# Passage from attention to the expert tiles: eight pieces of work put in another order or on another engine

## The reference, cut to what matters

```python
attn_out = _mha(x, in_proj_w, in_proj_b, out_proj_w, out_proj_b)
x = _layernorm(x + attn_out, ln1_g, ln1_b)
gp = softmax(xt @ w_group + b_group); g_idx = argmax(gp)          # 4 groups
ep_sel = softmax of the 2 experts of that group; e_idx_local = argmax
combine = one_hot(flat_e, 8) * (g_prob * e_prob)
h = relu(xt @ w1[e] + b1[e]); y = h @ w2[e] + b2[e]; out = combine @ y
x = _layernorm(x + moe_out, ln2_g, ln2_b)                          # and the input x is added
```

## Time and profile before

| | us |
|---|---|
| median of 3 runs | 595.16 |
| lowest, highest | 593.21, 599.90 |
| the profiled execution: its time | 594.82 |
| the profiled execution: its span | 593.0 |
| self-attention's last turn ends, first tile's result on DVE (in the span) | about 492, 506.1 |

### The profile page before, as it was taken

One profiled execution on the slowest core, in us unless ns is written; L12 is line 12 of the kernel. 1 busy time (PEld: TensorE's weight loads), 2 busy tenths in 40 slices (PEclk: granted clock), 3 DMA queues, 4 the chain that ended last, 5 costly groups with the idle time before them and its releaser, 6 DMA issues. The chain is left out here.

```text
span 593.0 us, 14386 instructions
## 1 busy us (share of the span) xinstructions
PE 517.6 (87%) x4673; PEld 345.3 (58%) x4673; DVE 430.0 (73%) x1165; ACT 396.4 (67%) x1109; POOL 286.7 (48%) x511
## 2 busy tenths in 40 slices
PE   6888799999999999989799998999998757987780
PEld 4656466777666666654455555555555436766660
DVE  3697978888888888857455678686777758955662
ACT  4456578877887888885576776766776544656660
POOL 0577742222222222020533568686786462766564
PEclk9997999999999999999999999999999898689886
DMA  8600999999996000000100000101220043243410
GB/s 331 270 2 30 278 269 275 272 272 274 272 275 176 0 0 0 2 1 4 34 2 2 1 3 29 38 29 45 103 97 28 29 118 83 78 126 96 106 39 10
DMA packets 48534, 60.76 MB, mean 102 GB/s; under 512 B 2488, under 2 KB 45509, under 8 KB 47574
## 3 DMA queue, kind: packets, MB, share of 16 engines
q1 hardware_dynamic: 45686, 53.59, 33.2%
q0 software_dynamic: 2784, 6.37, 3.1%
HBM read 18.30 MB, written 42.10 MB: 102 GB/s over the span
## 5 line engine op out<-in xcount | busy, mean ns | idle before, releaser
L1567 DVE TENSOR_REDUCE nm<-SC 128x8 f32<-128x1024 f32 x64 | 75.3, 1219 | 30.4 <-PE SC L1076 29.8
L1464 DVE TENSOR_REDUCE room_w<-SC 128x512 f32<-128x2048 f32 x32 | 73.3, 2290 | 13.7 <-PE SC L927 13.7
L2081 ACT ACTIVATE room_p<-ST 128x1024 f32<-128x1024 f32 x64 | 62.1, 1021 | 22.8 <-PE ST L1094 22.8
L600 POOL TENSOR_TENSOR spread<-parts,units 128x48 bf16<-128x48 bf16 x32 | 8.8, 275 | 122.8 <-DVE parts L1454 122.8
L1987 ACT ACTIVATE room_w<-room_w,shift 128x128 f32<-128x128 f32 x128 | 49.8, 391 | 20.6 <-DVE shift L1471 20.4
L798 POOL DMA_INDIRECT out<-room_v,id_r x39 | 39.2, 1004 | 23.9 <-DVE room_v L1915 13.8
L1978 ACT ACTIVATE room_w<-ST,cv 128x128 f32<-128x128 f32 x128 | 36.5, 367 | 17.3 <-PE ST L942 17.2
L1113 PE MATMUL SC<-room_p,room_w 128*32 128x128 f32 x1024 | 35.6, 281 | 7.6 <-DVE room_w L1592 4.1
L942 PEld LDWEIGHTS ST<-room_w 128*128 128x128 f32 x256 | 33.1, 191 | 15.4 <-issue 13.0
L2088 ACT ACTIVATE room_w<-SC 128x512 f32<-128x512 f32 x32 | 19.1, 598 | 33.9 <-PE SC L1113 33.1
L1996 ACT ACTIVATE room_w<-room_w,inv 128x128 f32<-128x128 f32 x128 | 41.0, 409 | 0.6 <-DVE inv L1476 0.6
(11 more groups left out here) (297 smaller groups left out, 1401.2 us busy)
## 6 DMA issues: line engine op xcount, KB each, us to landing
sorted_rows<-w SPq DMA_DIRECT2D x8, 4290.0 KB, 42.2
room_v<-sorted_rows SPq DMA_DIRECT2D x39, 130.0 KB
x_t<-xT SPq DMA_DIRECT2D x2, 1024.0 KB, 8.1
ctx_t<-adj SPq DMA_DIRECT2D x1, 2048.0 KB, 17.3
room_w<-x SPq DMA_DIRECT2D x8, 256.0 KB, 2.9
room_w<-mask SPq DMA_DIRECT2D x1, 1536.0 KB
w<-weights SPq DMA_DIRECT2D x1, 1228.0 KB, 8.5
x_t<-w SPq DMA_DIRECT2D x1, 1032.0 KB, 6.4
```

The source lines that it names most:

```text
L1464: dve.tensor_reduce(logit[:, :, :], SC[:, :, :].rearrange("p b (i m) -> p b m i", i=TYPES), AX_X, ALU.max)\
L1567: dve.tensor_reduce(nm[:, v % 2, 2 * PER_R * pair:2 * PER_R * (pair + 1)], SC[:, 2 * pair:2 * pair + 2, :].rearrange("p r (i n) -> p (r i) ...
L2081: act.activation(ex[:, v % 2, 2 * pair:2 * pair + 2, :], ST[:, 2 * pair:2 * pair + 2, :], ACT.Exp)\
```

## The change

1. POOL: `rows_x(6)`, until now on DVE at the end of turn 31, is done by POOL in `rest(0)`.
2. DVE: `first_taken` moves from the end of turn 31 to the end of turn 29.
3. DVE: `norm1_logits(6)` and links 0 to 5 move from turn 32 behind `normalise(31)`, `residual_out(29)` and its statistics; links 6 to 11 move from there behind `residual_out(30)`.
4. DVE: `norm1_logits(7)` moves from `rest(3)` to ahead of `rows_x1(6)`.
5. PE: the rank product of group 6 moves from turn 1 to turn 2 of the tile pipeline, behind the first tile's `ht`.
6. ACT: `norm1_out(6)` moves behind the copy of the first tile, `gate_exps(6)` to the end of turn 2.

```diff
 # GpSimd
             def rest(k):
+                if k == 0:
+                    rows_x(G - 2)
                 if k == 1:
                     norm1_power(G - 1)
 # TensorE
             def ranks(k):
-                if k == 1:
+                if k == 2:
                     pe.wait_ge(S("route_chain"), (G - 3) * ROUTE + RANK_LINK)
                     rank(G - 2, False)
...
-                if k == 1:
+                if k == 2:
                     ranks(k)
 # VectorE
-                if b == 0 and normed:
+                if b == 0 and normed and u < B:
                     norm1_logits(norm)
                     route(norm, range(0, 6))
...
-                if u == B - 1:
-                    rows_x(G - 2)
+                if u == B - GB + 1:
                     first_taken()
             def rest(k):
...
                     norm1_stats(B - 3)
-                    route(G - 2, range(6, 12))
+                    norm1_logits(G - 2)
+                    route(G - 2, range(0, 6))
                 if k == 1:
                     residual_out(B - 2)
                     norm1_stats(B - 2)
+                    route(G - 2, range(6, 12))
                 if k == 2:
...
                     route(G - 2, range(12, SLOT_LINK))
+                    norm1_logits(G - 1)
                     rows_x1(G - 2)
                 if k == 3:
-                    norm1_logits(G - 1)
                     route(G - 2, range(SLOT_LINK, ROUTE))
 # ScalarE
                 if k == 1:
                     heads_turned(B - 1)
+
+            def later_rest(k):
+                if k == 1:
                     norm1_out(G - 2)
+                if k == 2:
                     gate_exps(G - 2)
-            def later_rest(k):
```

## The result

| | before | after |
|---|---|---|
| median of 20 runs each, us | 594.38 | 597.14 |
| lowest, highest | 592.13, 599.90 | 591.91, 600.23 |
| profiled execution: time, span | 594.82, 593.0 | 594.2, 592.4 |

The ratio is 1.0041, 95% interval 1.0022 to 1.0059: slower by 2.4 us (0.0041 x 594.38), against +0.8 forecast. The case within 1% came true, and so did the wide range of 590.5 to 600.0 us; on the forecast's base the ratio gives 597.3 us (1.0041 x 594.82), just above its own range of 594.5 to 597. The profiled pair shows the opposite sign, 592.4 against 593.0 us, and can't be read by its spans: the executions differ in the tile loop by more than the change does. The profiled execution of the changed kernel is also 2.9 us faster than its median. So the passage is read by itself, from one place that the change doesn't touch, `residual_out(25)`, to DVE's first result.

What follows compares the result with a forecast made beforehand. No engine bounds throughout: DVE and PE lead by turns, nobody from 480 to 490. `first_taken` +1.30 and residuals -0.5, the rest 0, gave +0.8 on 594.82: 595.6 us; own range 594.5 to 597, wide range 590.5 to 600.0.

Steps and rivals of the forecast that it cites:

- The case within 1%: Whole kernel: time differs by no more than 1% (5.9 us), about what a measurement can tell; chance 0.89.
- `first_taken` to turn 29: DVE, ahead of `normalise(28)` and `residual_out(26)`: no cover while PE waits, cost between 0 and 1.30, taken as +1.30 us.
- Removing it moves nothing there.: DVE, end of turn 31: taking `first_taken` and `rows_x(6)` away gains nothing, since PE releases `normalise(30)` late anyway.
- the hole: After 484 us, PE idle 4.08 and DVE 3.96 us during POOL's scatters; on the path, seemingly tied to them.
- `rows_x(6)` to POOL: POOL's addition has ample cover: 0; ends +1.2, if it holds a DVE operation such as `norm1_logits(6)`, and -0.2.
- Residuals ahead of routing: DVE, turn 32 and `rest(0)`: reordering removes the 0.51 us break before `residual_out(31)`; -0.5 us, between 0 and -0.6.
- Rank later: PE issues the rank 0.9 us later, with slack 0.4 before DVE asks for it: 0, at worst +1.3.
- rival C: The later rank product blocks DVE and costs 1.3 us: 596.9; chance 0.10.
- ACT, 0, its wait below 1 us: ACT gets `shift1` about 1.8 us earlier, its 1.73 us wait falls below 1; 0 for the end, at best -0.5.
- Rival A: `first_taken` and `rows_x` delayed `normalise(30)`: removal gains 1.98 us, 593.6; with the hole gone too, 589.5; chance 0.22.
- Rival B: Tile loop: one DVE wait for PE more (599.0) or less (592.2), chance 0.13; two or more (602.4), 0.05.
- Rival D: First tile's copy comes earlier, nothing else; within the forecast's 0.50 chance; without DVE's 0.5 it gives 596.1.

Runs made afterwards that it cites:

- e6: Kernel before with only `first_taken` moved to the end of turn 29 and done four times there; ratio to the kernel before 1.0105.
- e10: Changed kernel with `first_taken` back at the end of turn 31, run again on the third chip; ratio to the kernel before 0.9939.
- e9: Kernel before with only `first_taken` moved to the end of turn 29, run again on the third chip; ratio to the kernel before 1.0030.
- e1: Changed kernel with `first_taken` back at the end of turn 31, all other parts kept; ratio to the kernel before 1.0003.
- e2: Kernel before with only `first_taken` moved to the end of turn 29, `rows_x(6)` left on DVE; ratio to the kernel before 0.9992.
- e12: Changed kernel with POOL's additions for group 5 waiting for link 11 and for the end of `first_taken`, third chip; ratio to the kernel before 0.9989.
- e11: Changed kernel with POOL's additions for group 5 waiting until link 11 is done, third chip; ratio to the kernel before 1.0003.
- e4: Kernel before with SP issuing the loads of the last rows ahead of the loads of the first 13 tiles; ratio to the kernel before 0.9996.
- e7: Changed kernel with `first_taken` back, POOL's group 5 additions behind link 11, and last rows loaded ahead of the first 13 tiles; ratio to the kernel before 0.9979.
- e5: The changed kernel measured once more, unaltered, on another chip; ratio to the kernel before 1.0039.
- e8: Changed kernel with `first_taken` back in turn 31 and POOL's group 5 additions behind link 11; 590.32 us, ratio to the kernel before 0.9922.

## Why the prediction was right or wrong

The case within 1% was right, and it had 0.89: any small change would have met it. The amount wasn't right, +2.4 us against +0.8, and that the first result of the profiled pair came as near as +1.4 is in part luck: the clock's 1.16 us were missing from the sum, and a hole shorter by 0.33 us and a `weigh(31)` faster by 0.61, which weren't foreseen either, took most of them back.

**`first_taken` to turn 29, +1.30.** Right in place, in sign and in that nothing covers it: PE's idleness went from 1.07 to 2.48, and e6's repeats each come out in full. This is the term that was mis-sized. Two things were left out. First, PE's longer idleness costs its clock: a mean of 0.57 granted in turn 31, products of 2.09 us instead of 1.14, in all 1.16 us up to the last residual product (1.15 to `weigh(31)` between e10 and e9). Second, where the links end early, an operation of `first_taken` is itself held by POOL, and the idleness grows by 2.4 (1.19 to 3.55) and not by 1.4. The passage is then 3.4 us longer (e1 to e2; 3.3 from e10 to e9), and 1.4 in the other case (before to after). The measured 2.4 lies between, but that it is a mixture of the two isn't shown: no profile of the kernel before falls in the early case, and only profiled executions tell the case.

**"Removing it moves nothing there."** Nearly right on the chips with the hole: in e1, with `first_taken` back, DVE is idle another 1.03 us ahead of `normalise(30)`. Where `weigh(31)` ran at full clock PE was less late. DVE is idle 1.53 us there in the changed kernel, less than the 1.98 us that were taken away, and 0.74 in e2, less than the 1.30 of `first_taken`; the differences, 0.4 and 0.6 us, are an estimate of what the removal paid.

**`rows_x(6)` to POOL, 0.** Right for the changed kernel: L676 occurs seven times, and the moved one (493.77 to 495.03) holds nothing of DVE. e12 shows the upper end (+1.2) once the timing shifts: `norm1_logits(6)`'s first operation takes 1.23 us instead of 0.15.

**Residuals ahead of routing, -0.5.** Half right. From the statistics of batch 28 to the first result it is 12.60 us before (493.46 to 506.06) and 12.34 after (495.63 to 507.97): -0.26. The 0.51 us ahead of `residual_out(31)` went, but `normalise(31)` now waits 0.25 for PE.

**Rank later, 0.** Right, rival C out. The ranks start at 500.94 and DVE reads them at 501.63 with no wait:

```profile
500.94 0.18 PE L1158 MATMUL ST<-oh_h,before_h 128*128 128x32 bf16 x1
```

```profile
501.63 0.19 DVE L1685 TENSOR_TENSOR rk<-ST,oh_h 128x32 f32<-128x32 f32 x1
```

**ACT, 0, its wait below 1 us.** The 0 holds, but the sign that was forecast, a wait under 1 us, wasn't seen. ACT in the changed kernel:

```profile
503.83 1.65 ACT L2110 ACTIVATE room_w<-room_w,shift,rstd 128x128 f32<-128x128 f32 x4 [1.59 <-DVE room_w L1716]
```

The wait went from 1.73 to 1.59 only. The wait of the earlier trace rows was for `shift1`, as I had read it. That was ready at 503.0 now, and the one left is for the first operation of `rows_x1(6)`, which ends later: `norm1_out(7)` overwrites what that reads, and waits for its semaphore `x1g_ready` too. I had left that second wait out. PE's wait for the second relu is 2.10 instead of 2.39.

**Rival A, the cover was real.** Not on the first chips. On the third, with no hole, `first_taken` at its old place ends at 487.0 in e10 and `normalise(30)` starts at 487.1, 2.42 us behind the start of `weigh(31)`; in e9, e11 and e12, without it, it is 1.80 or 1.81. So it cost 0.6 us there, as the rival has it; but the move costs more: e9 is 1.0030. **Rival B, more collisions.** Not seen in the profiled pair: the waits of DVE for L1321 sum to 11.7 us in the tile loop against 13.0, one of 3.8 us on "remote" beside them. On the third chip the tile loop is equal within 0.04 us, so B is out there; on the others the profiled executions spread by 3.7 us behind the table (74.0 to 77.7), and a share of B in the 2.4 us isn't excluded. **Rival D** is in the forecast and was right: counted from the statistics of batch 28, the first tile's `ht` starts 0.7 us earlier (4.76 instead of 5.43), and that does nothing for the end.

**What stays open.** Why e10 gains 0.6% on the third chip where the same code gave 1.0003 on the first: there is no profile of the kernel before on that chip. Of the 5.0 us between the medians of e9 and e10 the passages account for 3.3, and the profiled execution of e10 is the slowest of its seven. What makes the hole, and why one chip shows none. And where 1.0 us of the 2.4 lies.

## What to carry to other kernels

Price a moved piece by who already waits behind its new place: where PE stood idle for DVE, each added microsecond of DVE came out in full (e6), and the longer idleness cost PE another 1.15 us through its clock (e9, e10). Before putting small VectorE operations anywhere, look at which GpSimd additions run beside them; here ordering POOL behind the chain of links gave 0.9952, where the whole rearrangement gave 1.0041, and with the rearrangement less `first_taken` it gave 0.9922. A wait that a change makes vanish in one kernel may stand unchanged in the next (e4 and e7): try a cause in two kernels before believing it. A stall that looks as if it would swallow a delay may be tied to the delayed work: double or quadruple the work and see whether the stall shrinks.

## What the runs showed that I had not expected

- VectorE operations with one tensor in SBUF are held too: `TENSOR_SCALAR` over 128x8 with constants took 1.18 us in e5 and 1.13 in e11, a cast of 128x4 0.78 us in e8, each beside a POOL addition of 1.26 to 1.29 us, against 0.17 to 0.20 alone. A memset of 0.06 us in e11 (477.18) ran unheld beside the addition that then held the next tensor operation for 1.20. The page "SBUF — State Buffer" of the Trainium skill, in the section named above, gives the exclusion for two SBUF inputs and for a 2-port mode; whether the tiny operations with one input run in a 2-port mode no run here shows.
- PE's releases can be seen late around POOL's indirect DMAs, with SP's tile loads beside them (before, after, e8) or without (e7): DVE's `normalise` started 2.7 us (before) and 3.4 us (after) behind the end of the PE product it needs, and 0.03 in e10. In e7 ACT's copy started 2.96 us behind the end of `weigh(31)`. The cause stays open. One chip of the three showed none of it in four profiles, and ran the kernel before in 573.7 instead of 593.8 us; 60.2 us of its profiles lie behind the table of the later tiles, where the others have 74.0 to 77.7.
